# One tap of a depthwise 3x3 conv goes from VectorE to ScalarE and GpSimd (a two-layer Mamba and attention kernel on one Trainium2 core)

## The chip, the cores and the metric

The kernel runs on one core of a Trainium2 chip. Its time is the device time of one execution in microseconds (us). The core has five engines that work beside one another and wait for each other by semaphores: TensorE (PE, with its weight loads as PEld), VectorE (DVE), ScalarE (ACT), GpSimd (POOL) and SyncE (SP), which issues most of the DMAs. Here GpSimd issues some DMAs too. All data are float32.

## The reference, cut to what matters

Two layers work on x of shape (2, 768, 64, 64). The change lies in layer 0, which widens 768 channels to 1536 and sends them through a depthwise 3x3 conv, Silu, a selective scan along all 4096 positions, a norm over channels and a projection back:

```python
x = hs @ in_proj_w.T
xs = jnp.transpose(x, (0, 3, 1, 2))
xs = jax.lax.conv_general_dilated(xs, conv_w, (1, 1), ((1, 1), (1, 1)),
                                  feature_group_count=1536, ...) + conv_b[None, :, None, None]
xs = xs * jax.nn.sigmoid(xs)
...
delta = softplus(dt @ dt_w + dt_b);  dA = exp(delta * A);  dBu = delta * u * B
states = scan(dA, dBu)               # 4 states per channel
y = sum over states of (states * C) + D * u
out = layernorm(y) @ out_proj_w.T
```

Each output of the conv is a sum of nine taps: a weight of the channel times the input, shifted by -1, 0 or 1 rows and columns. Layer 1 (an attention with statistics of tokens) has no conv.

## The kernel before, in words

**Tiles, chunks and slots.** A chunk is 8 image rows, that is N = 512 positions, of one image; there are NCH = 16 chunks, 8 for each of the two images. A chunk has K = 12 tiles of 128 channels, so layer 0 has NT = 192 tiles of 128 x 512. The work is a software pipeline written out by hand: each engine runs a loop over slots S, and in slot S works on several tiles at once, each a fixed number of slots behind. In slot S, TensorE projects tile S (L564) and ScalarE copies the result from PSUM into the padded window buffer win_v (L743, with two rows kept as halo, L739 and L747). The conv of tile S - 2 runs on ScalarE and VectorE, its last adds (tile S - 3) on GpSimd. From tile S - 16 on the scan follows: du and g_ring on GpSimd, decays on ScalarE, scans and products with C on VectorE, the sum over states on GpSimd in S - 18. The projection back (L580, on TensorE) and its evacuation on VectorE (L945, L952, in odd slots) belong to an earlier chunk.

**The conv before the change.** ScalarE multiplies the centre tap and adds the bias, from win_v into PSUM p_cv (L768). VectorE adds six taps one after the other, each a multiply and add over 128 x 512 (`tap`, L938): five into p_cv, the last from p_cv into uy. TAPS (L418) names the six: all but the centre and (2, 1), (2, 2). These two are multiplied on ScalarE by the weight, into two buffers of conv_part (`product`, L713 to L716), and added to uy on GpSimd (L876, L879). Three of VectorE's taps stand ahead of scans 2 and 3 of the slot and the others behind the products with C of these.

**The order on each engine around it.** An engine takes its instructions in order, so what waits holds up what stands behind it.
- ScalarE, slot S: centre tap (L768), square (L774), product 0, skip (L785), product 1, state copy (L711), decays 2 and 3 (L706), then, by the slot, the load of the next chunk, Silu (every fourth slot) or softplus (every fourth), the copy to win_v, state copy, decays 0 and 1 of the next tile. Product n waits until GpSimd's add n of the tile before has read the buffer (L714). In one slot of each chunk x_dbl is copied in two steps (L779, L792) with a product on TensorE between them (L570), and goes out to memory and back as B_bc.
- GpSimd, slot S: an accumulating DMA (L871, waits for VectorE's products with C of the slot before), the two conv adds (L876, waits for VectorE's last tap; L879 waits for L876), du (L883), g_ring for all four states (L889), then two sums (L893 waits for the DMA, L897).
- VectorE, slot S: scans 0 and 1 (L917), products with C (L923), the evacuation if the slot is odd, three taps, scans 2 and 3, products with C, three taps, and once a chunk four operations of the norm.
- SyncE's queue loads weights and residuals and writes results; it waits for s_ct and s_tap only once, ahead of the last chunk's weights.

Silu of four tiles (L825) waits for the adds of all of them by the count of s_conv.

Of the kernel before, what the change touches and what calls it, by code (L numbers as in the profile page):

```python
# [18 lines left out]
ACT = mybir.ActivationFunctionType  # L19
AX = mybir.AxisListType  # L20

P = 128
# [4 lines left out]
def wait(eng, sem, value):  # L27

    if value > 0:
        eng.wait_ge(sem, value)  # L30
# [122 lines left out]
def layer0(nc, g):  # L153
# [6 lines left out]
    with ExitStack() as ctx:  # L160
        def sb(name, shape):
            return ctx.enter_context(nc.sbuf_tensor(name, shape, F32))

        cwt = sb("conv_w", [P, K, 9])
# [120 lines left out]
        NW, NO, NV, NX, NG, ND = 2, 2, 3, 2, 3, 5  # L285
# [14 lines left out]
        DU = sb("du", [P, N])  # L300
        SQ = sb("sq", [P, 2, N])
        LS = sb("ln_sums", [P, N])
        CT = sb("conv_part", [P, 2, N])
        RS = sb("ln_rstd", [P, N])
        XD = sb("x_dbl", [P, N])
        JK = ctx.enter_context(nc.sbuf_tensor("sq_out", [P, N], mybir.dt.bfloat16))
# [55 lines left out]
        def chunk_at(S, rel):  # L362
            c, r = divmod(S - rel, K)
            return c if r == 0 and 0 <= c < NCH else None
# [50 lines left out]
        def ucol(i):  # L415
            return UY[:, i % NU, :]

        TAPS = [(dy, dx) for dy in range(3) for dx in range(3) if (dy, dx) not in ((1, 1), (2, 1), (2, 2))]  # L418

        def last_bank(m):  # L420
            return (p_in[:], p_cv[:], p_dt[:, 0, :], p_dt[:, 1, :], p_op[:], p_ln[:])[m]
# [7 lines left out]
        def win_view(i, dy, dx):  # L429
            return VS[:, i % NV, dy:dy + ROWS, dx:dx + W]  # L430

        def rows(ap):
            return ap.rearrange("p (r w) -> p r w", w=W)
# [6 lines left out]
        with nc.Block() as block:  # L440
            @block.sync
            def _(sp):
# [17 lines left out]
                for S in range(SLOTS):  # L460
                    if S == 0:
                        load_x(sp, 0)
                    load_win(S + NW - 1)
                    for n in (2 * S, 2 * S + 1):
                        if n < NPIECE:
                            t, k = divmod(n, CPB)
                            wait(sp, s_st, n - 3)
                            sp.dma_start(stage(n), XTR[1, :, t, k * N:(k + 1) * N]).then_inc(s_xs[n % 4], 16)
                    if S >= S_OP:
                        load_wout(S - S_OP + 1)  # L470
                    r = out_at(S, S_OV - 1)
                    if r is not None:
                        c, m = divmod(r, XT)
                        b, k = divmod(c, CPB)
                        if r >= NX:
                            sp.wait_ge(s_xrs[r % NX], 16 * (r // NX))
                            sp.wait_ge(s_bn, r - NX + 1)
                        sp.dma_start(XR[:, r % NX, :], XTR[b, :, m, k * N:(k + 1) * N])\
                          .then_inc(s_xrl[r % NX], 16)
                    r = out_at(S, S_OV + 2)  # L480
                    if r is not None:
                        c, m = divmod(r, XT)
                        b, k = divmod(c, CPB)
                        sp.wait_ge(s_ov, r + 1)
                        sp.dma_start(x1_d[b, :, m, k * N:(k + 1) * N], XR[:, r % NX, :])\
                          .then_inc(s_xrs[r % NX], 16)
                    if S % K == K - 1 and S < NT - 1:
                        load_x(sp, (S + 1) // K)
                    c = chunk_at(S, S_XP[2] + 1)
                    if c is not None:  # L490
                        sp.wait_ge(s_xd, c + 1)
                        sp.dma_start(bc_d[c], XD[R:R + 2 * NS, :]).then_inc(s_bw, 16)
                        sp.wait_ge(s_bw, 16 * (c + 1))
                        wait(sp, s_dbu, K * c)
                        sp.dma_start(BB[:].rearrange("p n t -> p (n t)"),
                                     bc_d[c, 0:NS].rearrange("n t -> (n t)").partition_broadcast(P))\
                          .then_inc(s_b, 16)
                    c = chunk_at(S, 16)
                    if c is not None:
                        for h in range(2):  # L500
                            wait(sp, s_cm, NS * K * c - 2 + 2 * h)
                            sp.dma_start(CB[:, 2 * h:2 * h + 2].rearrange("p n t -> p (n t)"),
                                         bc_d[c, NS + 2 * h:NS + 2 * h + 2].rearrange("n t -> (n t)")
                                         .partition_broadcast(P)).then_inc(s_c[h], 16)
                    if S == NT + 2:
                        sp.wait_ge(s_inp, NT)
                        sp.wait_ge(s_tap, len(TAPS) * NT)
                        sp.wait_ge(s_ct, 2 * NT)
                        for m in range(4):
                            dst = WOA[:, m] if m < 2 else WOB[:, m - 2]  # L510
                            sp.dma_start(dst, woc_d[m]).then_inc(s_wol, 16)
                    if S == S_PAIR:
                        sp.wait_ge(s_op, 2 * XT * (CL - 1))
                        for m in range(XT):
                            sp.dma_start(last_x(m), XTR[B - 1, :, m, T - N:T]).then_inc(s_xll, 16)
# [174 lines left out]
            def _(act):  # L690
# [20 lines left out]
                    nc.scalar.activation(ST[:, i % K, 2 * p:2 * p + 2], p_da[:, :, N - 1], ACT.Copy).then_inc(s_scp, 1)  # L711

                def product(i, n):  # L713
                    wait(act, s_conv, 2 * (i - 1) + n + 1)  # L714
                    nc.scalar.activation(rows(CT[:, n]), win_view(i, 2, 1 + n), ACT.Copy,  # L715
                                         scale=cwt[:, i % K, 7 + n:8 + n]).then_inc(s_ct, 1)  # L716

                def row_out(i):
                    wait(act, s_tap, len(TAPS) * (i - NV + 1))
                    wait(act, s_ct, 2 * (i - NV + 1))  # L720
                    act.wait_ge(s_row, first_rows(i))
                    nc.scalar.activation(VS[:, i % NV, 1, 1:1 + W], p_in[:, 0:W], ACT.Copy).then_inc(s_rowev, 1)

# [8 lines left out]
                def evacuate(i):  # L732
                    c, j = divmod(i, K)
                    k = c % CPB
                    wait(act, s_tap, len(TAPS) * (i - NV + 1))
                    wait(act, s_ct, 2 * (i - NV + 1))
                    if k > 0:
                        act.wait_ge(s_hout, houts(i - K))
                        nc.scalar.activation(VS[:, i % NV, 0:2, 1:1 + W], HA[:, j], ACT.Copy)\  # L739
                          .then_inc(s_hin, 1)  # L740
                    act.wait_ge(s_inp, i + 1)
                    nr = ROWS - 1 if k == CPB - 1 else ROWS
                    nc.scalar.activation(VS[:, i % NV, 2:2 + nr, 1:1 + W], rows(p_in[:, 0:nr * W]), ACT.Copy)\  # L743
                      .then_inc(s_vev, 1)
                    if k < CPB - 1:
                        wait(act, s_hin, hins(i))
                        nc.scalar.activation(HA[:, j], rows(p_in[:, N - 2 * W:N]), ACT.Copy).then_inc(s_hout, 1)  # L747

                for S in range(SLOTS):
# [10 lines left out]
                    b = tile(S, L_CONV)  # L760
# [25 lines left out]
                          .then_inc(s_skip, 1)  # L786
                    if b is not None:
                        product(b, 1)
                    c = chunk_at(S, S_XP[2] + 1)
                    if c is not None:  # L790
                        act.wait_ge(s_xf, c + 1)
# [28 lines left out]
                                             accum_out=sq1[:, bb, m * CPB + k:m * CPB + k + 1]).then_inc(s_bn, 1)  # L820
                    if S >= 6 and S % 4 == 2 and (S - 6) // 4 < NT // 4:
                        q = (S - 6) // 4
                        act.wait_ge(s_conv, 8 * (q + 1))
                        o = UY[:, 4 * q % NU:4 * q % NU + 4, :]
                        nc.scalar.activation(o, o, ACT.Silu).then_inc(s_silu, 1)  # L825
                        nc.scalar.preload_act_table_set(EXPSET)
# [36 lines left out]
            def _(pool):  # L863
                nc.gpsimd.memset(VS, 0.0).then_inc(s_pad, 1)
                pool.wait_ge(s_pad, 1)
                for S in range(SLOTS):
# [4 lines left out]
                        nc.gpsimd.dma_start(gi[:, 0:2], gi[:, 2:4], accum_op=ALU.add).then_inc(s_ns1[y % NG], 16)  # L871
                    b = tile(S, L_CONV + 1)
                    if b is not None:
                        pool.wait_ge(s_ct, 2 * b + 1)
                        pool.wait_ge(s_tap, len(TAPS) * (b + 1))
                        nc.gpsimd.tensor_tensor(ucol(b), ucol(b), CT[:, 0], ALU.add).then_inc(s_conv, 1)  # L876
                        pool.wait_ge(s_ct, 2 * b + 2)
                        pool.wait_ge(s_conv, 2 * b + 1)
                        nc.gpsimd.tensor_tensor(ucol(b), ucol(b), CT[:, 1], ALU.add).then_inc(s_conv, 1)  # L879
                    if i is not None:  # L880
                        pool.wait_ge(s_delta, i + 1)
                        wait(pool, s_dbu, i)
# [16 lines left out]
                    if i is not None:  # L899
                        k, j = (i // K) % CPB, i % K  # L900
                        if j < NV and k in (0, CPB - 1):
                            wait(pool, s_tap, len(TAPS) * (i - NV + 1))
                            wait(pool, s_ct, 2 * (i - NV + 1))
                            nc.gpsimd.memset(VS[:, i % NV, 0 if k == 0 else ROWS + 1, :], 0.0).then_inc(s_zero, 1)

            @block.vector
# [895 lines left out]
```

## Time and profile before

| | us |
|---|---|
| median of 3 runs | 3775.08 (3770.55 to 3781.36) |
| the profiled execution | 3775.21 |
| its span, first to last instruction | 3773.4 |
| layer 0's slots with scan and conv adds | about 253 to 2602 of the span |
| busy in the span: PE, DVE, ACT, POOL | 3440.0, 2915.9, 2353.5, 2344.4 |

A row of the trace names the engine, the source line (L876), the operation, and the tile written and the tiles read. Busy time is the time in which an engine had an instruction at work. The times in a timeline are counted from the span's first instruction, in us. A figure in brackets at a row's end is the idle time before it and what ended that.

### The profile page before, as it was taken

Reading aid. Unit: us, or ns where it says so; the run is one execution under the profiler, and the core shown is the slowest. Engines: PE = TensorE matmul, PEld = TensorE weight load, DVE = VectorE, ACT = ScalarE, POOL = GpSimd, SP = SyncE. Lnnn points to the kernel's source line nnn. Section 1 sums busy time; section 2 is a strip of 40 time slices with the busy share of each in tenths; the row PEclk is TensorE's granted clock in tenths of the full one; section 3 lists DMA queues with packets and bytes.
Section 4 is the critical chain, followed back from the end, with each engine's and each line's share of the span. In section 5 each row is a group of like instructions: output and inputs, shape, how many; then the busy total and the mean of one; then the engine's idle time right before and its main releaser. Section 6 shows DMA issues by size and latency. Waiting matters only on the chain. (4 is left out here: it accounts for less than half of the span.)

```text
span 3773.4 us, 39046 instructions
## 1 busy us (share of the span) xinstructions
PE 3440.0 (91%) x10696; PEld 1731.0 (46%) x10696; DVE 2915.9 (77%) x4082; ACT 2353.5 (62%) x4094; POOL 2344.4 (62%) x1557
## 2 busy tenths in 40 slices
PE   4876799999999899999999999997879999999999
PEld 4422233333334344333333333332337867767787
DVE  4469999999999989999999999998743345555532
ACT  1356777788777767777777777777534555432211
POOL 0148888898889978988888889888820001112111
PEclk7888899999999999999999999998999999999999
DMA  7244455655556544555555555555532223356564
GB/s 281 88 143 107 102 139 132 166 137 144 145 130 170 131 126 133 144 147 146 150 134 144 147 147 149 136 140 156 130 108 78 65 82 99 111 185 198 198 195 154
DMA packets 217034, 529.85 MB, mean 140 GB/s; under 512 B 24728, under 2 KB 45784, under 8 KB 213872
## 3 DMA queue, kind: packets, MB, share of 16 engines
q1 hardware_dynamic: 173808, 376.32, 31.7%
q0 software_dynamic: 43008, 151.02, 18.3%
q8 instruction: 88, 1.44, 0.2%
q14 instruction: 130, 1.06, 0.1%
HBM read 346.11 MB, written 80.48 MB: 113 GB/s over the span
## 5 line engine op out<-in xcount | busy, mean ns | idle before, releaser
L564 PE MATMUL p_in<-xn,win_v 128*128 128x512 f32 (+1 forms) x2304 | 1062.5, 610 | 103.2 <-ACT halo L747 64.7
L580 PE MATMUL p_op<-uy,wout_ring 128*128 128x512 f32 x2160 | 1019.9, 622 | 83.4 <-DVE x_res L952 83.4
L917 DVE TENSOR_TENSOR_SCAN p_da<-p_da,state,g_ring 128x512 f32<-128x512 f32 x672 | 827.4, 1277 | 110.2 <-ACT p_da L706 74.6
L889 POOL TENSOR_TENSOR g_ring<-du,B_bc 128x2048 f32<-128x2048 f32 x192 | 870.6, 4534 | 15.9 <-DMA B_bc<-bc_scratch 0.9
L938 DVE SCALAR_TENSOR_TENSOR p_cv<-win_v,conv_w,p_cv 128x512 f32<-128x512 f32 x960 | 723.0, 753 | 88.5 <-ACT p_cv L768 67.5
L564 PEld LDWEIGHTS p_in<-xn,win_v 128*128 128x128 f32 x2304 | 442.2, 197 | 696.2 <-issue 696.2
L580 PEld LDWEIGHTS p_op<-uy,wout_ring 128*128 128x128 f32 x2160 | 413.5, 198 | 680.0 <-issue 568.1
L706 ACT ACTIVATE p_da<-delta,A 128x512 f32<-128x512 f32 x768 | 499.5, 682 | 12.5 <-ACT state L711 0.2
L923 DVE TENSOR_TENSOR g_ring<-p_da,C_bc 128x512 f32<-128x512 f32 x768 | 487.3, 676 | 0.0
L1370 PE MATMUL banks<-x_split,w_split 128*128 128x512 f32 x1152 | 464.2, 403 | 24.1 <-DMA ident<-in_ident_d 19.9
L1372 PE MATMUL banks<-x_split,w_split 128*128 128x512 f32 x1152 | 452.0, 392 | 0.0
L1371 PE MATMUL banks<-x_split,w_split 128*128 128x512 f32 x1152 | 451.5, 392 | 0.0
L876 POOL TENSOR_TENSOR uy<-uy,conv_part 128x512 f32<-128x512 f32 x192 | 256.0, 1333 | 259.2 <-DVE uy L938 259.2
L1215 POOL DMA_DIRECT2D q_scratch<-q_ring x96 | 51.9, 540 | 535.9 <-DVE q_ring L1635 535.7
L715 ACT ACTIVATE conv_part<-win_v,conv_w 128x512 f32<-128x512 f32 x384 | 273.4, 715 | 15.2 <-POOL uy L876 5.1
L1370 PEld LDWEIGHTS banks<-x_split,w_split 128*128 128x128 f32 x1152 | 218.0, 189 | 116.9 <-issue 38.9
L879 POOL TENSOR_TENSOR uy<-uy,conv_part 128x512 f32<-128x512 f32 x192 | 244.5, 1273 | 29.0 <-POOL uy L876 2.2
L711 ACT ACTIVATE state<-p_da 128x2 f32<-128x2 f32 x384 | 65.3, 170 | 304.3 <-DVE g_ring L923 301.9
L897 POOL TENSOR_TENSOR uy<-uy,g_ring 128x512 f32<-128x512 f32 x192 | 243.8, 1270 | 15.1
L893 POOL TENSOR_TENSOR g_ring<-g_ring 128x512 f32<-128x512 f32 x192 | 244.1, 1272 | 12.4 <-DMA g_ring<-g_ring 12.3
L883 POOL TENSOR_TENSOR du<-delta,uy 128x512 f32<-128x512 f32 x192 | 248.7, 1295 | 0.0
L1223 POOL DMA_DIRECT2D out<-x_ring x96 | 51.8, 540 | 311.1 <-DVE x_ring L1579 305.8
(212 smaller groups left out, 4283.6 us busy)
## 6 DMA issues: line engine op xcount, KB each, us to landing
g_ring<-g_ring POOLq DMA_DIRECT2D x192, 512.0 KB, 5.6
win_v<-in_win SPq DMA_DIRECT2D x192, 384.0 KB, 3.1
wout_ring<-wout_scratch SPq DMA_DIRECT2D x184, 384.0 KB, 4.0
x_ring<-x_scratch SPq DMA_DIRECT2D x192, 256.0 KB, 2.7
q_scratch<-q_ring POOLq DMA_DIRECT2D x96, 256.0 KB, 2.4
x_split<-q_scratch SPq DMA_DIRECT2D x96, 256.0 KB, 3.3
out<-x_ring POOLq DMA_DIRECT2D x96, 256.0 KB, 2.9
x_res<-in_x SPq DMA_DIRECT2D x90, 256.0 KB, 4.6
```

The lines of the kernel that those rows point to most:

```text
L564: last = nc.tensor.matmul(p_in[:, 0:n], WR[:, i % NW, t, :], XN[:, t, off:off + n], start=(t == 0), stop=(t == XT - 1))
L580: last = nc.tensor.matmul(p_op[:], OR[:, e % NO, k - h * HALF, :], ucol(c * K + k), start=(k == 0), stop=(k == K - 1))
L706: nc.scalar.activation(p_da[:, n % 2, :], DL[:, i % ND, :], ACT.Exp, scale=At[:, j * NS + n:j * NS + n + 1]).then_inc(s_da, 1)
L715: nc.scalar.activation(rows(CT[:, n]), win_view(i, 2, 1 + n), ACT.Copy, scale=cwt[:, i % K, 7 + n:8 + n]).then_inc(s_ct, 1)
L876: nc.gpsimd.tensor_tensor(ucol(b), ucol(b), CT[:, 0], ALU.add).then_inc(s_conv, 1)
L889: nc.gpsimd.tensor_tensor(G[:, i % NG], DU[:].unsqueeze(1).broadcast_to([P, NS, N]), BB[:], ALU.mult).then_inc(s_dbu, 1)
L917: nc.vector.tensor_tensor_scan(bank, bank, G[:, i % NG, n, :], init, ALU.mult, ALU.add)\
L923: nc.vector.tensor_tensor(G[:, i % NG, n], p_da[:, n % 2, :], CB[:, n], ALU.mult).then_inc(s_cm, 1)
L938: nc.vector.scalar_tensor_tensor(rows(dst), win_view(i, dy, dx), cwt[:, j, 3 * dy + dx:3 * dy + dx + 1], rows(p_cv[:]), ALU.mult, ALU.add) ...
L1370: nc.tensor.matmul(bank(m), WX[:, m, q, 0, :], hi(h), start=(q == 0), stop=False)
L1371: nc.tensor.matmul(bank(m), WX[:, m, q, 0, :], lo(h), start=False, stop=False)
L1372: last = nc.tensor.matmul(bank(m), WX[:, m, q, 1, :], hi(h), start=False, stop=(q == XT - 1))
```

## The change

The tap (2, 0) is taken out of VectorE's list and becomes a third product on ScalarE and a third add on GpSimd. TAPS then holds (0, 0), (0, 1), (0, 2), (1, 0) and (1, 2); VectorE runs three of them ahead of scans 2 and 3 and two behind. The products are now those of (2, 0), (2, 1) and (2, 2), in this order; the third follows the second directly on ScalarE. conv_part gets a third buffer of 128 x 512, and the counts of s_ct and s_conv go from two to three a tile.

```diff
-        CT = sb("conv_part", [P, 2, N])
+        CT = sb("conv_part", [P, 3, N])
...
-        TAPS = [(dy, dx) for dy in range(3) for dx in range(3) if (dy, dx) not in ((1, 1), (2, 1), (2, 2))]
+        TAPS = [(dy, dx) for dy in range(3) for dx in range(3) if (dy, dx) != (1, 1) and dy < 2]
...
                 def product(i, n):
-                    wait(act, s_conv, 2 * (i - 1) + n + 1)
-                    nc.scalar.activation(rows(CT[:, n]), win_view(i, 2, 1 + n), ACT.Copy,
-                                         scale=cwt[:, i % K, 7 + n:8 + n]).then_inc(s_ct, 1)
+                    wait(act, s_conv, 3 * (i - 1) + n + 1)
+                    nc.scalar.activation(rows(CT[:, n]), win_view(i, 2, n), ACT.Copy,
+                                         scale=cwt[:, i % K, 6 + n:7 + n]).then_inc(s_ct, 1)
...
                     if b is not None:
                         product(b, 1)
+                        product(b, 2)
...
-                        act.wait_ge(s_conv, 8 * (q + 1))
+                        act.wait_ge(s_conv, 12 * (q + 1))
...
                     if b is not None:
-                        pool.wait_ge(s_ct, 2 * b + 1)
                         pool.wait_ge(s_tap, len(TAPS) * (b + 1))
-                        nc.gpsimd.tensor_tensor(ucol(b), ucol(b), CT[:, 0], ALU.add).then_inc(s_conv, 1)
-                        pool.wait_ge(s_ct, 2 * b + 2)
-                        pool.wait_ge(s_conv, 2 * b + 1)
-                        nc.gpsimd.tensor_tensor(ucol(b), ucol(b), CT[:, 1], ALU.add).then_inc(s_conv, 1)
+                        for n in range(3):
+                            pool.wait_ge(s_ct, 3 * b + n + 1)
+                            wait(pool, s_conv, 3 * b + n)
+                            nc.gpsimd.tensor_tensor(ucol(b), ucol(b), CT[:, n], ALU.add).then_inc(s_conv, 1)
```

The other edits are the same count of s_ct, 3 in place of 2 a tile, where ScalarE, GpSimd and SyncE wait for a window buffer to come free.

## Rows read from the trace of the kernel before

**Rows 1.** The page: busy tenths of VectorE, ScalarE and GpSimd in 40 slices of the span.

```profile
DVE  4469999999999989999999999998743345555532
ACT  1356777788777767777777777777534555432211
POOL 0148888898889978988888889888820001112111
```

**Rows 2.** Windows, one steady chunk: stretch, length, busy time of each engine, PE clock, DMA.

```profile
1847.40:2004.60 157.20, 150.03 (x392) 59.22 (x391) 149.84 (x193) 124.16 (x215) 139.72 (x84) 0.98 0.55 144
```

**Rows 3.** Waits in that chunk: engine, tile, line <- releaser: us, times, longest.

```profile
POOL uy L876 <- DVE uy L938: 9.2, 9, 1.2
...
DVE p_da L917 <- ACT p_da L706: 5.3, 4, 2.1
POOL g_ring L871 <- DVE g_ring L923: 4.7, 3, 2.6
...
PE p_op L580 <- DVE x_res L952: 4.0, 1, 4.0
```

**Rows 4.** Timeline of GpSimd, one slot without a wait: start, us, engine, line.

```profile
1934.88 0.86 POOL L871 DMA_DIRECT2D g_ring<-g_ring  x1
...
1937.19 1.29 POOL L879 TENSOR_TENSOR uy<-uy,conv_part 128x512 f32<-128x512 f32 x1
...
1946.83 0.87 POOL L871 DMA_DIRECT2D g_ring<-g_ring  x1
```

**Rows 5.** Timeline of GpSimd behind the last conv add.

```profile
2602.47 4.53 POOL L889 TENSOR_TENSOR g_ring<-du,B_bc 128x2048 f32<-128x2048 f32 x1
...
2611.76 4.51 POOL L889 TENSOR_TENSOR g_ring<-du,B_bc 128x2048 f32<-128x2048 f32 x1
```

**Rows 6.** Groups of instructions by line: xcount | busy us, mean ns | idle before.

```profile
L938 DVE SCALAR_TENSOR_TENSOR p_cv<-win_v,conv_w,p_cv 128x512 f32<-128x512 f32 x960 | 723.0, 753 | 88.5 <-ACT p_cv L768 67.5
...
L715 ACT ACTIVATE conv_part<-win_v,conv_w 128x512 f32<-128x512 f32 x384 | 273.4, 715 | 15.2 <-POOL uy L876 5.1 <-POOL uy L879 2.6
...
L879 POOL TENSOR_TENSOR uy<-uy,conv_part 128x512 f32<-128x512 f32 x192 | 244.5, 1273 | 29.0 <-POOL uy L876 2.2
```

**Rows 7.** Timeline of GpSimd: L889 of tiles 0, 12, 80 and 96, two adds.

```profile
252.96 4.52 POOL L889 TENSOR_TENSOR g_ring<-du,B_bc 128x2048 f32<-128x2048 f32 x1 [0.93 <-DMA B_bc<-bc_scratch]
259.54 1.27 POOL L876 TENSOR_TENSOR uy<-uy,conv_part 128x512 f32<-128x512 f32 x1 [2.06 <-DVE uy L938]
260.95 1.27 POOL L879 TENSOR_TENSOR uy<-uy,conv_part 128x512 f32<-128x512 f32 x1
...
413.12 4.54 POOL L889 TENSOR_TENSOR g_ring<-du,B_bc 128x2048 f32<-128x2048 f32 x1
...
1301.36 4.56 POOL L889 TENSOR_TENSOR g_ring<-du,B_bc 128x2048 f32<-128x2048 f32 x1
...
1533.85 4.54 POOL L889 TENSOR_TENSOR g_ring<-du,B_bc 128x2048 f32<-128x2048 f32 x1
```

**Rows 8.** Timeline of ScalarE in the slot of rows 4: second product, first decay behind it.

```profile
1938.52 0.72 ACT L715 ACTIVATE conv_part<-win_v,conv_w 128x512 f32<-128x512 f32 x1
...
1939.33 1.30 ACT L706 ACTIVATE p_da<-delta,A 128x512 f32<-128x512 f32 x2
```

**Rows 9.** Timeline of VectorE: scans 2 and 3, products with C, taps behind them.

```profile
1929.38 2.46 DVE L917 TENSOR_TENSOR_SCAN p_da<-p_da,state,g_ring 128x512 f32<-128x512 f32 x2
1931.74 1.27 DVE L923 TENSOR_TENSOR g_ring<-p_da,C_bc 128x512 f32<-128x512 f32 x2
1932.93 1.54 DVE L938 SCALAR_TENSOR_TENSOR p_cv<-win_v,conv_w,p_cv 128x512 f32<-128x512 f32 x2
```

**Rows 10.** Timeline of GpSimd during the second image's norm.

```profile
382.88 0.88 POOL L871 DMA_DIRECT2D g_ring<-g_ring  x1 [9.66 <-DVE g_ring L923]
```

**Rows 11.** Waits from 1270 to 1470 us, where the second image begins.

```profile
POOL g_ring L871 <- DVE g_ring L923: 26.4, 8, 6.7
```

**Rows 12.** Windows, around TensorE's wait in the chunk (columns as rows 2).

```profile
1914.60:1921.20 6.60, 5.51 (x7) 2.41 (x8) 6.49 (x10) 2.85 (x7) 4.45 (x3) 0.50 0.00 0
```

More of the change, by code:

```diff
@@ L507, in _ @@
                         sp.wait_ge(s_tap, len(TAPS) * NT)
-                        sp.wait_ge(s_ct, 2 * NT)
+                        sp.wait_ge(s_ct, 3 * NT)
                         for m in range(4):
@@ L713, in product @@
                 def product(i, n):
-                    wait(act, s_conv, 2 * (i - 1) + n + 1)
-                    nc.scalar.activation(rows(CT[:, n]), win_view(i, 2, 1 + n), ACT.Copy,
-                                         scale=cwt[:, i % K, 7 + n:8 + n]).then_inc(s_ct, 1)
+                    wait(act, s_conv, 3 * (i - 1) + n + 1)
+                    nc.scalar.activation(rows(CT[:, n]), win_view(i, 2, n), ACT.Copy,
+                                         scale=cwt[:, i % K, 6 + n:7 + n]).then_inc(s_ct, 1)
                 def row_out(i):
                     wait(act, s_tap, len(TAPS) * (i - NV + 1))
-                    wait(act, s_ct, 2 * (i - NV + 1))
+                    wait(act, s_ct, 3 * (i - NV + 1))
                     act.wait_ge(s_row, first_rows(i))
@@ L735, in evacuate @@
                     wait(act, s_tap, len(TAPS) * (i - NV + 1))
-                    wait(act, s_ct, 2 * (i - NV + 1))
+                    wait(act, s_ct, 3 * (i - NV + 1))
                     if k > 0:
@@ L902, in _ @@
                             wait(pool, s_tap, len(TAPS) * (i - NV + 1))
-                            wait(pool, s_ct, 2 * (i - NV + 1))
+                            wait(pool, s_ct, 3 * (i - NV + 1))
                             nc.gpsimd.memset(VS[:, i % NV, 0 if k == 0 else ROWS + 1, :], 0.0).then_inc(s_zero, 1)
```

## The prediction, made before the changed kernel ran

> **What bounds the kernel now.** I read the page first, for the split of the span. VectorE runs at nine tenths or more through almost all of layer 0 (about the first 2800 us) and GpSimd at eight tenths or more; layer 1 behind it is TensorE's and has no conv [rows 1]. So the change is worth what it does in layer 0.
>
> Then I looked at one steady chunk of 12 channel tiles, by the windows. The schedule repeats: a chunk takes 157.2 us, 13.1 us a slot. VectorE is busy for 149.8 of these, TensorE 150.0, GpSimd 139.7, ScalarE 124.2 [rows 2]. Which of them is the limit is told by the waits of the same chunk: VectorE waits 5.3 us for ScalarE's decays and for hardly anything else, while GpSimd waits 9.2 us for VectorE's last tap and 4.7 us for VectorE's products with C, and TensorE waits 4.0 us for VectorE once [rows 3]. VectorE sets the pace; GpSimd follows it with only 9.2 + 4.7 = 13.9 us of idle time in 157.2. Its other 143.3 us are 11.94 us a slot.
>
> That GpSimd is that close is seen in its timeline too. In one slot it has no wait at all, and from one L871 to the next 1946.83 - 1934.88 = 11.95 us go by [rows 4]: two conv adds, du, the 4.5 us product g_ring, two sums, and the issue of its own DMA. At the end of layer 0, where no conv is left, the same sequence without the two adds takes 2611.76 - 2602.47 = 9.29 us from one L889 to the next [rows 5]. Two adds are thus worth 2.66 us, 1.33 each.
>
> **The change part by part.**
>
> VectorE loses one tap in six per tile. In the grouped lines a tap is 753 ns [rows 6], so 12 x 0.75 = 9.0 us a chunk; its busy time falls from 149.8 to 140.8 us. That is the whole gain, and only if nothing else needs the 157.2.
>
> ScalarE gains one product per tile, 715 ns [rows 6]: 12 x 0.715 = 8.6, 124.2 to 132.8 us a chunk. As work it is covered by ScalarE's idle 33 us; without that cover it would cost 8.6 a chunk.
>
> GpSimd gains one add per tile, and here the price has to be chosen. The lines give 1273 ns for the second add [rows 6]. The timeline gives more: from the start of the first add to that of the second more goes by where the first starts late (259.54 to 260.95, 1.41 [rows 7]), since each add waits for the semaphore of the one before. The lower end is 1.27 (the busy time), the upper 1.41, and the 1.33 of the tail lies between. I take 1.41, because the new add sits in the middle of a row of adds on the same buffer, as that second one does. GpSimd's floor is then 11.95 + 1.41 = 13.36 us a slot, 160.3 a chunk: more than the 157.2 of now.
>
> (The Trainium skill, Perfetto Trace Analysis, section GPSIMD Engine Instruction, says that the reported spans of GpSimd don't add up and that start-to-start spacing is to be used. By the span the floor would be 13.22 a slot, 25 us less over the 178 slots below; by its rule it is 13.36. The rows at hand favour the rule: the spacing is 1.41 where the span says 1.27.)
>
> The wait that is added: product 2 on ScalarE needs its buffer back, so it waits for GpSimd's third add of the tile before, in the same slot. Queued behind it are the state copy L711 and decays 2 and 3 (L706), for which VectorE's scans 2 and 3 wait. Counted from GpSimd's L871 as T: the second add ends at 1937.19 + 1.29 - 1934.88 = T + 3.6 [rows 4], so the third at T + 5.0; product 0.72 later, T + 5.75; decay 2 starts 0.81 after the product's start [rows 8] and takes 0.65, so scan 2 can start at about T + 6.7. Two scans (2.4), two products with C (1.2) and the taps left behind them, two now instead of three (1.5), follow on VectorE without a pause [rows 9]: the last tap ends at T + 11.8. GpSimd's next slot begins at T + 13.36. The wait therefore has about 1.5 us to spare in an ordinary slot and is costed at nothing there; the cover is GpSimd's own longer slot. In a slot where ScalarE has more to do (softplus, and once a chunk x_dbl, for which it also waits for TensorE) the decays can come later than that by more than the slack. What then stays of GpSimd's idle time no row of before shows; it lies between 0 and the 13.9 us a chunk of now. I take 1.2 a chunk (an estimate), near the low end, because VectorE's 140.8 lie 19 under the new floor of 160.3 and most of the 13.9 was time that GpSimd waited for VectorE.
>
> Edits at nothing: the third buffer of conv_part (no transfer), the renumbered waits (Silu waits for the same tile, which product 2 has already waited for), the order of the taps. No DMA is added on SP or GpSimd; the DMA of L871 has one add more of time to land.
>
> The sum, over the slots in which GpSimd has conv adds and g_ring both: 178, from tile 0's L889 at 252.96 to tile 178's at 2602.47 [rows 5, 7], now 2349.5 us.
> - Tiles 0 to 12, now 160.2 [rows 7]: the floor of 160.3, and a wait of 9.66 us for the second batch's norm [rows 10] of which VectorE's new slack takes some 1.5: 168, +8.
> - Tiles 12 to 80, now 888.2 [rows 7]: 68 x 13.36 = 908.5, and 6 x 1.2: 915.7, +27.
> - Tiles 80 to 96, now 232.5 [rows 7], where the second batch begins: TensorE has first rows to do as well, and GpSimd waits 26.4 us there at L871 alone [rows 11]. 16 x 13.36 = 213.8 fits under it: 0.
> - Tiles 96 to 178, now 1068.6: 82 x 13.36 = 1095.5, and 7 x 1.2: 1103.9, +35.
> Together +70 us. Before tile 0 and behind tile 178 GpSimd is not the limit or has no conv: 0. The profiled execution took 3775.2 us, within 0.1 us of the median, so 3845.
>
> **Rivals.**
>
> Faster: GpSimd fits into the shorter slot. It decides where the new add costs under 13.9 / 12 = 1.16 us, for then GpSimd stays under 157.2 and VectorE's 9.0 us can come out, up to what TensorE (150.0 busy) lets go: at most 7.2 a chunk, over the 12.5 chunks outside tiles 80 to 96 some 90, so 3685, more likely half, 3730. Against it: no row here has such an add under 1.27, and the slot without a wait shows no gap to hide it in. Chance 0.03.
>
> No change: the add goes just into GpSimd's idle time. 12 x 1.27 = 15.3 against 13.9 would give +1.4 a chunk, +17 in all, and with some gain at the ends within 0.3% (11 us, about what a measurement of this kernel can tell). It needs every idle microsecond to go and the short price; 3785. Chance 0.05.
>
> Slower by far: the waits stay. If GpSimd kept its idle time of now in every slot, each of 178 slots would grow by 1.41: +251, 4026. Half of it, 3900, could come from the new wait on ScalarE (should the decays come later than T + 6.7, VectorE's last tap is late and GpSimd waits again), or from TensorE: its granted clock is 0.50, the lower level of 1.2 GHz, in the 6.6 us that begin during its 4.0 us wait [rows 12], and with more idle time it may fall more often, on 150 us of work in 161. For it: the two engines feed each other within a slot. Against: the 1.5 us to spare in each. Chance over 3895: 0.10.
>
> **How the numbers follow.** GpSimd as the pace setter has 0.82: slower by 28 to 120 us. The low end, 3803, is the floor by 1.33 and below, with no wait left (47 us for the floors by 1.41, less 178 x 0.08 = 14, less 5 at the norm). The high end, 3895, leaves some 5 us of idle a chunk. The rivals take the rest: 0.03 faster, 0.05 the same, 0.10 far slower. Faster 0.03, same 0.05, slower 0.92.
>
> **What would show it.** Right: from one L889 to the next 13.3 to 13.4 us in most slots; a chunk of 160 to 163; GpSimd busy near 155 us of it; the waits of L876 and L871 for VectorE almost gone, and in their place VectorE's scans waiting for g_ring or for decays, and ScalarE's L715 for GpSimd. VectorE's busy time down by 192 x 0.75 = 144 us in all, GpSimd's up by 244. Wrong: a chunk under 157, or GpSimd's waits for VectorE still at 10 us a chunk or more.

## The result, and the profile after

The changed kernel is slower: 3845.44 us (median of 4 runs, 3843.6 to 3849.26) against 3773.14 for the kernel before, a ratio of 1.0189 (95% interval 1.0171 to 1.0207). That is 72 us more. The profiled execution has a span of 3841.8 us.

The page's busy tenths of VectorE and GpSimd, in 40 slices (as [rows 1]):

```profile
DVE  4468888888888878889888888888753345555532
...
POOL 0259999999999989999999999999840001112111
```

The two engines have changed places: where VectorE stood at nine and GpSimd at eight, GpSimd now stands at nine through layer 0 and VectorE at eight.

A steady chunk, from tile 120's L889 to tile 132's, by the windows (columns as [rows 2]):

```profile
1893.10:2054.90 161.80, 152.09 (x392) 59.95 (x391) 141.57 (x182) 131.73 (x227) 155.16 (x97) 0.97 0.54 140
```

161.8 us instead of 157.2 [rows 2]. VectorE is busy 8.3 us less, ScalarE 7.6 more, GpSimd 15.4 more. The waits of the same chunk, first those of all engines, then GpSimd's alone (columns as [rows 3]):

```profile
DVE p_da L917 <- ACT p_da L706: 18.5, 9, 2.8
...
ACT conv_part L715 <- POOL uy L879: 10.2, 14, 1.5
```

```profile
POOL g_ring L872 <- DVE g_ring L923: 0.9, 1, 0.9
POOL uy L879 <- DVE uy L938: 0.4, 1, 0.4
```

GpSimd's 13.9 us of waits for VectorE [rows 3] are down to 0.9 + 0.4 = 1.3. Now VectorE is the one that waits, 18.5 us for decays (5.3 before), and ScalarE's products wait 10.2 us for GpSimd's adds. One slot of GpSimd in its timeline:

```profile
1900.19 0.87 POOL L872 DMA_DIRECT2D g_ring<-g_ring  x1
1900.80 4.39 POOL L879 TENSOR_TENSOR uy<-uy,conv_part 128x512 f32<-128x512 f32 x3
...
1913.56 0.89 POOL L872 DMA_DIRECT2D g_ring<-g_ring  x1
```

From one DMA issue to the next 13.37 us, with no wait, where [rows 4] had 11.95. The three adds now share line 879.

Where the 72 us are, by L889 of tiles 0, 12, 80, 96 and 178 (as [rows 5, 7]):

```profile
255.91 4.52 POOL L889 TENSOR_TENSOR g_ring<-du,B_bc 128x2048 f32<-128x2048 f32 x1 [0.49 <-DMA B_bc<-bc_scratch]
...
422.15 4.51 POOL L889 TENSOR_TENSOR g_ring<-du,B_bc 128x2048 f32<-128x2048 f32 x1
...
1338.81 4.55 POOL L889 TENSOR_TENSOR g_ring<-du,B_bc 128x2048 f32<-128x2048 f32 x1
...
1570.50 4.54 POOL L889 TENSOR_TENSOR g_ring<-du,B_bc 128x2048 f32<-128x2048 f32 x1
...
2675.32 4.52 POOL L889 TENSOR_TENSOR g_ring<-du,B_bc 128x2048 f32<-128x2048 f32 x1
```

| stretch | before | after | forecast for after |
|---|---|---|---|
| ahead of tile 0 | 253.0 | 255.9 | 253.0 |
| tiles 0 to 12 | 160.2 | 166.2 | 168 |
| tiles 12 to 80 | 888.2 | 916.7 | 915.7 |
| tiles 80 to 96 | 232.5 | 231.7 | 232.5 |
| tiles 96 to 178 | 1068.6 | 1104.8 | 1103.9 |
| behind tile 178, to the span's end | 1170.9 | 1166.5 | 1170.9 |

### The profile page after: what moved, and what is told of

It is laid out like the page before. It is cut to its first block and busy times, and to the rows that moved or that the text cites. A ratio compares the mean times of both kernels' runs of the same rounds, so it can differ in the third digit from the quotient of the medians.

```text
span 3841.8 us, 39430 instructions
## 1 busy us (share of the span) xinstructions
PE 3447.2 (90%) x10696; PEld 1731.4 (45%) x10696; DVE 2782.5 (72%) x3890; ACT 2473.5 (64%) x4286; POOL 2590.5 (67%) x1749
## 5 line engine op out<-in xcount | busy, mean ns | idle before, releaser
L564 PE MATMUL p_in<-xn,win_v 128*128 128x512 f32 (+1 forms) x2304 | 1081.4, 619 | 151.2 <-ACT halo L747 99.0
L580 PE MATMUL p_op<-uy,wout_ring 128*128 128x512 f32 x2160 | 1009.7, 617 | 65.3 <-DVE x_res L952 65.3
L879 POOL TENSOR_TENSOR uy<-uy,conv_part 128x512 f32<-128x512 f32 x576 | 777.4, 1350 | 180.1 <-DVE uy L938 122.5
L889 POOL TENSOR_TENSOR g_ring<-du,B_bc 128x2048 f32<-128x2048 f32 x192 | 869.9, 4531 | 15.6 <-DMA B_bc<-bc_scratch 0.7
L938 DVE SCALAR_TENSOR_TENSOR p_cv<-win_v,conv_w,p_cv 128x512 f32<-128x512 f32 x768 | 577.5, 752 | 95.2 <-ACT p_cv L768 80.9
L715 ACT ACTIVATE conv_part<-win_v,conv_w 128x512 f32<-128x512 f32 x576 | 405.1, 716 | 154.5 <-POOL uy L879 146.7
L1370 PEld LDWEIGHTS banks<-x_split,w_split 128*128 128x128 f32 x1152 | 217.2, 189 | 115.0 <-issue 36.7
L883 POOL TENSOR_TENSOR du<-delta,uy 128x512 f32<-128x512 f32 x192 | 248.8, 1296 | 0.0
L1372 PEld LDWEIGHTS banks<-x_split,w_split 128*128 128x128 f32 x1152 | 217.2, 189 | 47.0
L1371 PEld LDWEIGHTS banks<-x_split,w_split 128*128 128x128 f32 x1152 | 217.7, 189 | 42.2
```

The costliest lines, as they stand in the source:

```text
L564: last = nc.tensor.matmul(p_in[:, 0:n], WR[:, i % NW, t, :], XN[:, t, off:off + n], start=(t == 0), stop=(t == XT - 1))
L580: last = nc.tensor.matmul(p_op[:], OR[:, e % NO, k - h * HALF, :], ucol(c * K + k), start=(k == 0), stop=(k == K - 1))
L715: nc.scalar.activation(rows(CT[:, n]), win_view(i, 2, n), ACT.Copy, scale=cwt[:, i % K, 6 + n:7 + n]).then_inc(s_ct, 1)
L879: nc.gpsimd.tensor_tensor(ucol(b), ucol(b), CT[:, n], ALU.add).then_inc(s_conv, 1)
L889: nc.gpsimd.tensor_tensor(G[:, i % NG], DU[:].unsqueeze(1).broadcast_to([P, NS, N]), BB[:], ALU.mult).then_inc(s_dbu, 1)
L938: nc.vector.scalar_tensor_tensor(rows(dst), win_view(i, dy, dx), cwt[:, j, 3 * dy + dx:3 * dy + dx + 1], rows(p_cv[:]), ALU.mult, ALU.add) ...
```

## The experiments

Theory G: GpSimd's own instructions set the slot, at 13.36 us. The rivals: ScalarE's new product and what waits behind it set it (S), or VectorE still shares in it (V). Later runs take apart what is left over. All ratios are against the kernel before, run on the same chip in the same rounds. A ratio is good to about 0.15%, that is 6 us, and a difference between two runs to some 8 us.

**Leave out the add, keep the product.**

```diff
-                        for n in range(3):
+                        for n in range(2):
...
-                            wait(pool, s_conv, 3 * b + n)
+                            wait(pool, s_conv, 2 * b + n)
```

The counts that ScalarE waits for follow; product 2 then waits for the second add.

> GpSimd's third add is left out (the product of tap (2, 0) is still made on ScalarE, but not added). Theory G, GpSimd's own instructions set the slot: its slot goes back to 11.95 us, a chunk is then TensorE's and VectorE's, 151 to 154 us, and the time falls below both kernels, to some 3715 us (3690 to 3750). Rival S, ScalarE's new product and what waits behind it on ScalarE set the slot: the time stays at 3820 to 3845 us.

3739.95 us, ratio 0.9911 (0.9896 to 0.9926). 105 us thus hang on the add and what waits for it. The product without the add does not make the kernel slower, so S is out as the main cause. A chunk takes 154.5 us, just above the 151 to 154 expected.

**The add alone, with ScalarE's two products of before.** Against the changed kernel; the third add takes a buffer of zeros.

```diff
-                        product(b, 2)
...
+                nc.gpsimd.memset(CT[:, 2], 0.0).then_inc(s_pad, 1)
```

> GpSimd's third add alone: ScalarE makes the two products of before, and the third add takes a buffer of zeros that is written once, so that tap (2, 0) is missing from the result; VectorE has five taps as in the changed kernel. Theory G: 3838 to 3848 us, as the changed kernel. Rival S: without the third product and its wait the time falls to 3700 to 3775 us.

3823.28 us, ratio 1.0130 (1.0113 to 1.0147): 22 us under the changed kernel, so neither side is met to the letter. The chunk's two ends in GpSimd's timeline:

```profile
1879.61 4.53 POOL L889 TENSOR_TENSOR g_ring<-du,B_bc 128x2048 f32<-128x2048 f32 x1
...
2039.99 4.53 POOL L889 TENSOR_TENSOR g_ring<-du,B_bc 128x2048 f32<-128x2048 f32 x1
```

160.38 us, which is 12 x 13.36 with nothing over; the trace shows no wait of GpSimd in this chunk. That is G in its pure form: the add on GpSimd, and it alone, makes the floor. The 22 us on top in the changed kernel come with ScalarE's third product and its wait for the third add, of which the runs below tell more.

**VectorE keeps its sixth tap.**

```diff
-        TAPS = [(dy, dx) for dy in range(3) for dx in range(3) if (dy, dx) != (1, 1) and dy < 2]
+        TAPS = [(dy, dx) for dy in range(3) for dx in range(3) if (dy, dx) not in ((1, 1), (2, 1), (2, 2))]
```

> The changed kernel, but VectorE keeps all six taps (tap (2, 0) is counted twice). Theory G: VectorE's 9.0 us a chunk fit into its idle time, 3845 to 3865 us. Rival V, VectorE still shares in setting the slot: up to 178 x 0.75 = 134 us more, 3979 us.

3870.49 us, ratio 1.0257 (1.0241 to 1.0272). Only 25 of the 134 us that a sixth tap takes on VectorE reach the end, 5 more than G allowed. Most of them come in one place of the chunk: the slot behind the norm is 15.8 us long again, as in the kernel before, where it was 14.7 in the changed one. The slot ahead of it takes 13.8, and the other ten stay near 13.4. So what the change takes off VectorE is worth little once GpSimd is the longer one: V is a small part.

**The tap left out altogether**, on all engines: before's kernel with the TAPS of the changed one.

> The kernel before with tap (2, 0) left out of VectorE's list and put nowhere, so that it is missing from the result: what VectorE's saving is worth by itself. Run e1_no_third_add gave 3740 us with the third product still on ScalarE. If ScalarE's 0.72 us a tile costs what the step from the changed kernel (3845) to e2_add_alone (3823) says, some 20 us: 3715 to 3725 us. If that product costs nothing where GpSimd isn't the limit: 3735 to 3745 us.

3725.45 us, ratio 0.9875 (0.9860 to 0.9889). This is the most that taking one tap off VectorE could give with all else as it is: 48 us; 3.1 us a chunk (154.1) of the 9.0 that VectorE saves. The first run has ScalarE's product on top and took 3740, so the product costs 14.5 us there too: not hidden, though ScalarE is idle for 30 us of the chunk without it.

**du between the adds.** Each conv add waits for the one before it. du belongs to another tile and can stand between.

```diff
                             nc.gpsimd.tensor_tensor(ucol(b), ucol(b), CT[:, n], ALU.add).then_inc(s_conv, 1)
+                            if n == 0 and i is not None:
+                                pool.wait_ge(s_delta, i + 1)
+                                wait(pool, s_dbu, i)
+                                nc.gpsimd.tensor_tensor(DU[:], DL[:, i % ND, :], ucol(i), ALU.mult).then_inc(s_du, 1)
```

> The changed kernel with du (of another tile) moved between GpSimd's first and second add; nothing is added or left out. Theory G with the price of 1.41 us for an add that waits for the one before it: two of the waits on a result just written (add 2 on add 1, g_ring on du) are then covered, about 0.14 and 0.10 us a slot, and the time falls by 178 x 0.24 = 43 us, to 3802 us (3790 to 3815). If the 0.14 us is not a wait but part of each add: 3845 us. Rival S: 3845 us.

3839.93 us, ratio 1.0179 (1.0163 to 1.0194): 5 us where 43 were expected. By that number alone the 0.14 us would be no wait. But in the trace five of the twelve slots of a chunk did shrink to 13.05 us, more than expected, and others grew, to 14.3, 14.6 and 15.0. The second and third adds end 1.1 us later in the slot, and ScalarE's products waited for the adds 165.9 us in all, 146.7 in the changed kernel. What GpSimd gained seemed to be given back through ScalarE. The next two runs test that.

**Two buffers for products 1 and 2**, so that ScalarE waits there for adds of two tiles before. Product 0 keeps its one buffer.

```diff
-        CT = sb("conv_part", [P, 3, N])
+        CT = sb("conv_part", [P, 5, N])
...
-                    wait(act, s_conv, 3 * (i - 1) + n + 1)
+                    back = 1 if n == 0 else 2
+                    if i >= back:
+                        act.wait_ge(s_conv, 3 * (i - back) + n + 1)
```

> The changed kernel with two buffers each for the products of taps (2, 1) and (2, 2), by odd and even tiles, so that ScalarE's products 1 and 2 wait for GpSimd's adds of two tiles before and no longer for those of the same slot. Theory W, the 22 us between the changed kernel and e2_add_alone are this wait and the decays behind it: 3820 to 3828 us, every slot at 13.36 us. Rival P, they are the 0.72 us of the product itself on ScalarE: 3840 to 3847 us.

3833.24 us, ratio 1.0163 (1.0147 to 1.0178): between the two. In the steady chunk the long slot is nearly gone (13.5 us for 14.7), and the chunk takes 160.6 us. Of ScalarE's 22 us about 12 go with the wait and 10 stay, each good to some 8 us only. That the 10 are the product's own time is not shown: product 0 still waits.

**Both**, two buffers and du between.

> Both: two buffers as in e9_two_sets, and du between GpSimd's first and second add as in e3_du_between, where undisturbed slots took 13.05 us but others grew. Theory W, in e3 the third add came later and product 2 with it, so that the saving was given back: without the wait the floor of 12 x 13.05 = 156.6 us a chunk is reached or nearly, 3765 to 3790 us. Rival P: 3820 to 3840 us, as e3 within 20 us.

3792.84 us, ratio 1.0053 (1.0038 to 1.0068): 40 us under the same kernel without du between, just above the range for W and far from P. The steady chunk takes 157.4 us, 11 slots of 13.05 and one of 13.8. A slot of GpSimd's timeline (lines are shifted: L884 the adds, L888 du, L898 g_ring):

```profile
1893.93 0.88 POOL L877 DMA_DIRECT2D g_ring<-g_ring  x1
1894.54 1.58 POOL L884 TENSOR_TENSOR uy<-uy,conv_part 128x512 f32<-128x512 f32 x1
1895.77 1.57 POOL L888 TENSOR_TENSOR du<-delta,uy 128x512 f32<-128x512 f32 x1
1897.00 2.98 POOL L884 TENSOR_TENSOR uy<-uy,conv_part 128x512 f32<-128x512 f32 x2
1899.94 4.51 POOL L898 TENSOR_TENSOR g_ring<-du,B_bc 128x2048 f32<-128x2048 f32 x1
...
1906.97 0.87 POOL L877 DMA_DIRECT2D g_ring<-g_ring  x1
```

With du between, the starts are 1.23 us apart (1894.54, 1895.77, 1897.00), for none of these three waits for the one right ahead of it. The four instructions, three adds and du, take 5.40 us from the first one's start to g_ring's (1899.94), where the changed kernel takes 5.70 (1900.80 to 1906.50). The price of the order is thus shown, and so is the wait that hid it when du alone was moved.

**The same order in the kernel before.** du between its two adds.

> The kernel before with du between GpSimd's two adds, which takes some 0.3 us a slot of waits off GpSimd. If VectorE sets the pace before the change (theory G's starting point), only the few slots of 11.95 us gain, 0 to 1 us a chunk: 3760 to 3774 us. If GpSimd already shares in setting the pace everywhere: 178 x 0.3 = 53 us, 3720 us.

3802.34 us, ratio 1.0065 (1.0051 to 1.0079): slower by 25 us, which neither side had. From the instructions of line 715 (ScalarE's products), what they waited for, in us and times; first the kernel before, then this one:

```profile
  POOL uy L876: 5.1, 17
  POOL uy L879: 2.6, 6
```

```profile
  POOL uy L883: 105.5, 106
  POOL uy L876: 1.1, 2
```

The second add (L879 there, L883 here) comes later by du, product 1 waits for it, and the decays stand behind product 1. With two buffers for the second product:

```diff
-                    wait(act, s_conv, 2 * (i - 1) + n + 1)
+                    back = 1 + n
+                    if i >= back:
+                        act.wait_ge(s_conv, 2 * (i - back) + n + 1)
```

> e12_before_du (slower than the kernel before by some 25 us) with two buffers for the second product, so that ScalarE's product 1 waits for GpSimd's second add of two tiles before. Theory W, in e12 the second add came later by du and ScalarE's product 1, with decays 2 and 3 behind it, waited for it (L715 waited 105.5 us for it in all, 2.6 before): the loss goes, 3755 to 3775 us. Rival: VectorE's or TensorE's own wait for du or y, in their new order, is the cause: 3790 to 3805 us.

3776.83 us, ratio 1.0001 (0.9991 to 1.0011): the loss is gone (2 us over the stated range, level with the kernel before of the same rounds), so the wait was its cause. And GpSimd's shorter slot is worth nothing while VectorE sets the pace: the chunk is 157.2 us as before.

**Move the tap in some tiles only.** The counts of taps and products become sums over tiles; MOVED names the tiles of a chunk.

```diff
+        MOVED = (1, 3, 5, 7, 9, 11)
+
+        def nprod(i):
+            return 3 if i % K in MOVED else 2
+
+        def ntap(i):
+            return 8 - nprod(i)
```

> The tap moves only in the odd tiles of a chunk, six of twelve, whose slots on VectorE also have the evacuation of the projection; the even ones keep VectorE's sixth tap. Theory G: GpSimd's floor is 6 x 13.36 + 6 x 11.95 = 151.9 us a chunk, VectorE's busy time 145.3, TensorE's 150.0: 154 to 156 us a chunk, below both kernels, 3735 to 3760 us. If the engines can't even out a long slot with a short one, GpSimd's long slots add up with VectorE's: 3775 to 3810 us.

3787.04 us, ratio 1.0037 (1.0023 to 1.0052): in the range named for engines that can't even out. GpSimd's timeline at the longest slot, 1916.09 to 1932.47 (L894 the DMA, L901 the adds, L911 g_ring):

```profile
1916.09 4.51 POOL L911 TENSOR_TENSOR g_ring<-du,B_bc 128x2048 f32<-128x2048 f32 x1
...
1925.82 0.88 POOL L894 DMA_DIRECT2D g_ring<-g_ring  x1 [2.64 <-DVE g_ring L945]
1927.06 4.09 POOL L901 TENSOR_TENSOR uy<-uy,conv_part 128x512 f32<-128x512 f32 x3 [0.36 <-DVE uy L960]
...
1932.47 4.55 POOL L911 TENSOR_TENSOR g_ring<-du,B_bc 128x2048 f32<-128x2048 f32 x1
```

Tile 7 is moved, and its adds come right behind GpSimd's wait for VectorE's slow slot (the norm of the chunk), where nothing covers the added one: the slot takes 16.4 us, 15.8 in the kernel before. GpSimd's floor of 151.9 us and its 3.2 + 2.4 us of waits are the chunk's 157.5.

So the tiles were chosen by where GpSimd waited in the kernel before: MOVED = (3, 4, 5, 6), whose adds come ahead of that slot.

> The tap moves only in tiles 3, 4, 5 and 6 of a chunk, those between the slot of x_dbl and that of the norm, where GpSimd waited for VectorE in the kernel before (8.5 us of its 13.9); the others keep VectorE's sixth tap. Theory G: VectorE is 3.0 us earlier at the norm's slot and GpSimd's 5.6 us fit into its idle time there: up to 3 us a chunk less, 3735 to 3765 us. If what fits there is taken up by other waits, as in e6_odd_tiles: 3773 us or more.

3772.5 us, ratio 0.9987 (0.9978 to 0.9996): 0.1% faster, less than either end of what G expected (0.2% to 1%) and close to the rival's no gain. It is better than the six odd tiles by 0.5%, but it also moves fewer tiles, so that the choice of the tiles alone made the difference is not shown. The same tiles, with du between and two buffers for products 1 and 2:

> As e13_four, with du between GpSimd's first and second add and two buffers each for the products of taps (2, 2) and (2, 0), all computed as the reference has it. Theory G: with some 0.3 us a slot taken off GpSimd the chunk comes near the 154 us of e5_tap_dropped, 3720 to 3750 us. If du between the adds brings nothing where VectorE sets the pace: as e13_four within 5 us.

3758.47 us, ratio 0.9952 (0.9938 to 0.9966): faster than both kernels, the best complete version here, if 8 us short of the range. Which of the two additions brings it was not taken apart. The windows of its steady chunk:

```profile
1835.10:1990.90 155.80, 148.90 (x392) 58.75 (x391) 146.93 (x189) 125.74 (x220) 144.13 (x89) 0.99 0.55 146
```

155.8 us, with VectorE at 146.9, TensorE at 148.9 and GpSimd at 144.1: three engines within 5 us, so probably little is left to gain by moving work among them.

## Why the prediction was right

The forecast was 3845 us and +70; measured are 3845.44 and +72. The sum holds term by term as well, within 2 us in each stretch in which GpSimd has its adds; 2.9 us ahead of tile 0 and -4.4 behind tile 178, costed at nothing, nearly cancel; their causes were not looked into. Agreement to half a microsecond is luck: the steps below were good to some 5 us each.

**GpSimd's floor.** Forecast 13.36 us a slot, from 11.95 and a spacing of 1.41. Measured 13.37 in the changed kernel, and 160.38 us for a chunk in the run with the add alone. The choice of 1.41 over the 1.33 of the tail was right too: by the rows of the last section an add that need not wait for the one ahead adds 1.23 us and one that waits 1.41, together 2.64, and the two adds of before are one of each kind (2.66). The added one waits. The rule of the Trainium skill that was weighed (Perfetto Trace Analysis, GPSIMD Engine Instruction: take start-to-start spacing, not the span) points to this price as well, and the length of the slot agrees with it; by the span of 1.27 it would have been 25 us short (an estimate). But start to start the trace gives 1.41 only behind an add that itself has waited; from the first add of a slot to the second it gives 1.70.

**VectorE's gain.** 9.0 us a chunk were to be lost in idle time. VectorE's busy time fell by 8.3, and by 133 us over the span, where 144 were forecast (GpSimd's rose by 246, forecast 244). Putting the tap back costs 25 us of 134: right in the main. The cap of 90 us on the rival that GpSimd fits was far too generous: without the tap on any engine the gain is 48.

**The new wait.** Forecast: third product at T + 5.0, scans 2 and 3 from T + 6.7, last tap's end T + 11.8, with T GpSimd's DMA issue. In the slot with T = 1913.56, ScalarE's timeline has the third product and the decays behind it:

```profile
1918.63 0.72 ACT L715 ACTIVATE conv_part<-win_v,conv_w 128x512 f32<-128x512 f32 x1 [0.70 <-POOL uy L879]
1919.26 0.15 ACT L711 ACTIVATE state<-p_da 128x2 f32<-128x2 f32 x1
1919.44 1.30 ACT L706 ACTIVATE p_da<-delta,A 128x512 f32<-128x512 f32 x2
```

and VectorE's the scans, which wait for them, and the last tap:

```profile
1920.22 2.47 DVE L917 TENSOR_TENSOR_SCAN p_da<-p_da,state,g_ring 128x512 f32<-128x512 f32 x2 [2.52 <-ACT p_da L706]
...
1924.56 0.75 DVE L938 SCALAR_TENSOR_TENSOR uy<-win_v,conv_w,p_cv 128x512 f32<-128x512 f32 x1
```

T + 5.1, T + 6.7, and the last tap's end at T + 11.75. The wait fits into GpSimd's slot, as said.

**What is left over.** 1.2 us of GpSimd's idle time a chunk were assumed, for decays that come late where ScalarE has more to do; 1.3 are measured. In the sum that is 15.6 us over tiles 12 to 80 and 96 to 178, and there the changed kernel took 15.4 us longer than the run with the add alone (916.7 + 1104.8 against 909.7 + 1096.4). So this term is ScalarE's part of the loss, and its size, a guess between 0 and 13.9, came out by luck. GpSimd's wait stands in the slot behind the norm, but it begins two slots earlier, in one with softplus, as the prediction has it. First the changed kernel, then the run with the add alone:

```profile
1931.99 0.72 ACT L715 ACTIVATE conv_part<-win_v,conv_w 128x512 f32<-128x512 f32 x1 [0.70 <-POOL uy L879]
...
1938.39 1.26 ACT L729 ACTIVATE delta<-p_dt,cols 128x512 f32<-128x512 f32 x2 [0.85 <-PE p_dt L534]
...
1941.95 2.47 DVE L917 TENSOR_TENSOR_SCAN p_da<-p_da,state,g_ring 128x512 f32<-128x512 f32 x2 [2.07 <-ACT p_da L706]
...
1959.98 4.52 POOL L889 TENSOR_TENSOR g_ring<-du,B_bc 128x2048 f32<-128x2048 f32 x1
...
1967.99 0.88 POOL L872 DMA_DIRECT2D g_ring<-g_ring  x1 [0.93 <-DVE g_ring L923]
1969.23 4.10 POOL L879 TENSOR_TENSOR uy<-uy,conv_part 128x512 f32<-128x512 f32 x3 [0.36 <-DVE uy L938]
```

```profile
1923.45 1.26 ACT L729 ACTIVATE delta<-p_dt,cols 128x512 f32<-128x512 f32 x2 [0.86 <-PE p_dt L534]
...
1927.01 2.47 DVE L917 TENSOR_TENSOR_SCAN p_da<-p_da,state,g_ring 128x512 f32<-128x512 f32 x2 [2.07 <-ACT p_da L706]
...
1946.44 4.52 POOL L889 TENSOR_TENSOR g_ring<-du,B_bc 128x2048 f32<-128x2048 f32 x1
```

In the changed kernel the third product waits for its buffer ahead of softplus. (Softplus itself waits alike for TensorE in both, 0.85 and 0.86 us.) The decays behind softplus let VectorE's scans go 18.03 us ahead of this g_ring, 19.43 without the third product: 1.4 us later against GpSimd. From there VectorE runs through the norm without a pause, until GpSimd waits 0.93 + 0.36 us for it. What the prediction did put at nothing is the product as work, because ScalarE's 33 us of idle time cover it; a share of busy time can't show that. With two buffers about 10 of the 22 us stay, and where the add is left out the product costs 14.5, so it was not quite nothing.

**The rivals.** TensorE's clock did not make the time: the mean granted clock is 0.97 in the chunk, 0.98 before. In the slot with GpSimd's wait it falls to 0.50, the lower level (1962 to 1968 us), as it did in a slot of the kernel before [rows 12], behind a wait of 2.92 us of TensorE for VectorE; VectorE itself does not wait for TensorE there. The stretch of tiles 80 to 96, costed at nothing under TensorE's load, took 231.7 for 232.5.

## What to carry to other kernels

Before moving work to a second engine, divide the idle time of that engine in one period by the number of added instructions (here 13.9 / 12 = 1.16 us), and compare it with what one more such instruction adds to the engine's slot in the same chain (1.41), not with its span: where that is larger, the second engine becomes the limit, whatever the first one saves. Work put on an engine with idle time can still cost, if other engines wait for what stands behind it in that engine's queue; where it waits for a buffer, a second buffer can take that part away. Where the engines are close to each other, try to move only the pieces whose new work lands in the second engine's waits, and look where those are slot by slot; here that gained 0.1% by itself.

## What the runs showed of the hardware that was not expected

On GpSimd, a 128x512 add that waits for the result of the add right ahead of it ends 1.41 us behind that one's end; an instruction of that size that need not wait ends 1.22 to 1.23 us behind the one ahead. The three adds of the slot at T = 1900.19, one by one:

```profile
1900.80 1.56 POOL L879 TENSOR_TENSOR uy<-uy,conv_part 128x512 f32<-128x512 f32 x1
1902.50 1.27 POOL L879 TENSOR_TENSOR uy<-uy,conv_part 128x512 f32<-128x512 f32 x1
1903.92 1.27 POOL L879 TENSOR_TENSOR uy<-uy,conv_part 128x512 f32<-128x512 f32 x1
```

They end (start and span added) at 1902.36, 1903.77 and 1905.19, and du, which does not wait for them, 1.23 us later at 1906.42. The starts alone mislead: where an instruction need not wait, its start can be reported while the one ahead still runs, with a span of 1.56 to 1.58 us in place of 1.27, so that the first two adds start 1.70 us apart and the next two 1.42. The cost of such a wait, 0.18 us, is thus read from the ends or from the whole slot. Two of them covered by du (the second add's for the first, g_ring's for du) took 13.36 - 13.05 = 0.31 us off a slot.
